# Cross-attention of a Perceiver layer: products for the row maxima in 64-row tiles, one bank for keys and values

## The reference

```python
q = query_states @ Wq.T + bq        # 128 rows, from layernorm(x)
k = key_value_states @ Wk.T + bk    # 12544 rows
v = key_value_states @ Wv.T + bv
# 16 heads of 16, q scaled by 1/4
scores = jnp.einsum('bhqd,bhkd->bhqk', q, k)
attn = jax.nn.softmax(scores, axis=-1)
ctx = jnp.einsum('bhqk,bhkd->bhqd', attn, v)
x = x + ctx @ Wo.T + bo
```

## Time and profile before

| | us |
|---|---|
| median of 3 runs | 610.64 |
| lowest and highest | 609.08, 611.08 |
| profiled execution | 610.5 |
| its span in the trace | 608.7 |

### The profile page before, as it was taken

The page is one execution under the profiler, slowest core; times in us unless marked ns, Lnnn a source line. Parts: engine busy times, 40 slices in busy tenths (PEclk is TensorE's granted clock), DMA queues, the critical chain, the costliest instruction groups (busy, mean ns, idle before and its releaser), DMA issues.

```text
span 608.7 us, 15724 instructions
## 1 busy us (share of the span) xinstructions
PE 550.2 (90%) x6337; PEld 490.0 (81%) x6337; DVE 432.7 (71%) x808; ACT 333.1 (55%) x629; POOL 91.7 (15%) x74
## 2 busy tenths in 40 slices
PE   3777999999999999999999999999999986364997
PEld 3776999999899999999989999998987874233886
DVE  5689877777777777777777777777784255574674
ACT  2311666666666666666666666666667730042563
POOL 6641110110110111111101101101000000006000
PEclk9889999999999999999999999999999996585899
DMA  7989866866867878878778768677583059700000
GB/s 258 139 135 137 139 108 110 128 111 109 128 113 110 123 116 115 118 116 118 116 110 125 113 109 127 110 111 101 85 133 116 4 184 376 269 1 1 1 1 9
DMA packets 44507, 70.46 MB, mean 116 GB/s; under 512 B 6772, under 2 KB 14868, under 8 KB 44308
## 3 DMA queue, kind: packets, MB, share of 16 engines
q1 hardware_dynamic: 44436, 69.47, 63.4%
HBM read 30.56 MB, written 0.13 MB: 50 GB/s over the span
## 4 chain that ended last, share of the span: by engine, by line
PE 79%; DVE 9%; DMA 5%; SPq 3%; issue 2%; ACT 1%; DVEq 0%
PE bank L558 18%; PE bank L575 16%; PE bank L537 14%; PE bank L524 10%; PE bank L509 10%; PE bank L747 4%; DMA kT<-kst 4%; PE bank L763 2%; PE bank L494 2%; SPq L239 2%; DVE stepmax L853 1%; PE bank L590 1%; DMA ctxT<-in_ctxT 1%; DMA qmat<-maxT 1%; PE bank L488 1%
## 5 line engine op out<-in xcount | busy, mean ns | idle before, releaser
L853 DVE TENSOR_REDUCE stepmax<-bank 128x2 f32<-128x512 f32 x392 | 267.6, 690 | 98.2 <-PE bank L537 68.7
L376 ACT ACTIVATE probs<-bank 128x512 f32<-128x512 f32 x392 | 231.5, 598 | 151.1 <-PE bank L558 149.7
L537 PE MATMUL bank<-kT,qM 128*128 128x256 f32 x784 | 160.7, 287 | 9.0 <-DMA kT<-kst 7.3
L558 PE MATMUL bank<-qmat,kT 128*128 128x256 f32 x784 | 165.7, 297 | 1.9 <-DMA qmat<-maxT 1.5
L558 PEld LDWEIGHTS bank<-qmat,kT 128*128 128x128 f32 x784 | 119.3, 191 | 23.1 <-issue 18.5
L537 PEld LDWEIGHTS bank<-kT,qM 128*128 128x128 f32 x784 | 122.2, 192 | 11.6 <-DMA kT<-kst 8.4
L309 POOL TENSOR_TENSOR cparts<-ctxT,cparts 128x512 fp32r<-128x512 f32 x49 | 63.0, 1286 | 350.0 <-ACT cparts L355 350.0
L524 PE MATMUL bank<-wv,cparts 128*128 128x256 f32 x588 | 103.5, 287 | 2.7 <-DVE maxT L878 2.7
L509 PE MATMUL bank<-cparts,wk 128*128 128x256 f32 x588 | 104.9, 290 | 0.0
L575 PE MATMUL bank<-probs,val 128*17 128x128 f32 x3136 | 104.7, 274 | 0.0
L524 PEld LDWEIGHTS bank<-wv,cparts 128*128 128x128 f32 x588 | 85.4, 195 | 4.7 <-issue 4.7
(11 more groups left out here) (176 smaller groups left out, 311.6 us busy)
## 6 DMA issues: line engine op xcount, KB each, us to landing
kT<-kst SPq DMA_DIRECT2D x294, 128.0 KB, 4.6
ctxT<-in_ctxT SPq DMA_DIRECT2D x49, 256.0 KB, 5.3
w<-in_w SPq DMA_DIRECT2D x24, 512.0 KB, 10.0
bias<-in_biases SPq DMA_DIRECT2D x1, 1024.0 KB, 7.8
qmat<-maxT SPq DMA_DIRECT2D x26, 8.0 KB
const<-in_const SPq DMA_DIRECT2D x1, 262.0 KB, 4.9
w_xk<-in_w_xk SPq DMA_DIRECT2D x1, 256.0 KB, 3.3
w_xv<-in_w_xv SPq DMA_DIRECT2D x1, 256.0 KB, 3.7
```

Source lines behind the costliest of these rows:

```text
L376: act.activation(probs[k % PROBS][:, :, :], sc_bank[k % 3][:, :].rearrange("p (h q) -> p h q", q=P), ACT.Exp).then_inc(S["exp_ready"], 1)
L537: last = pe.matmul(mx_bank[p % 2][:, a * SK:(a + 1) * SK], qM[:, p, a, :], kT[:, n % RING, p, :], start=True, stop=True)
L558: last = pe.matmul(sc_bank[k % 3][:, i * 2 * P:(i + 1) * 2 * P], kT[:, n % RING, p, j * P:(j + 1) * P], qmat[b % 2][:, p, :, :], start=Tru ...
L853: dve.tensor_reduce(stepmax[:, n % BS, 2 * p:2 * p + 2], mx_bank[p % 2][:, :].rearrange("p (a k) -> p a k", a=2), AX_X, ALU.max).then_inc( ...
```

## The change

1. A maximum product takes only the 64 rows of its half (`qM[rows, ...]`, `kT[rows, ...]`). Four products form a group `g`: head pairs `2g` and `2g + 1`, and for each the lower and the upper 64 rows. Half `a` writes to bank `a` of the pair of banks `wide[g % 2]`, pair `i` to half `i` of that bank. A group stands in slots 0, 2, 4 and 6. `mx_done` is raised twice a group.
2. `step_max` reduces 128 x 1024 columns of a pair of banks to four maxima, four times a round. `stepmax` has the shape `[P, BS, 2, PAIRS]`, and `block_max` reads it so.
3. Banks 0 to 3 are the two pairs, bank 4 holds keys and values in turn, banks 5 and 6 the scores, bank 7 stays. `keys` waits for `val_ready` of the step before and for `mt_read`, `values` waits for `kl_ready` of its own step; `scores` waits for the exponential two slots back.
4. All 12 key products stand in slots 2 and 3, all value products in slots 6 and 7. `turn_max` moves from slot 2 to slot 1, `values_out` on VectorE to the front of slot 0, `max_turned` from slot 3 to slot 1, `keys_low` from slot 5 to behind the reduction in slot 4.

The uses of the banks in the set-up move along (`xnT`, the query projection and `qT` to banks 0 to 3); those lines are left out here.

```diff
-        k_bank, v_bank, mx_bank, sc_bank, pv_bank = B[0], B[1], B[2:4], B[4:7], B[7]
+        wide = [ctx.enter_context(nc.psum_tensor(f"wide{i}", [P, 2, 512], F32)) for i in range(2)]
+        B = [wide[i // 2][:, i % 2, :] for i in range(4)]
+        B += [ctx.enter_context(nc.psum_tensor(f"bank{i}", [P, 512], F32))[:, :] for i in range(4, 8)]
+        k_bank, v_bank, sc_bank, pv_bank = B[4], B[4], B[5:7], B[7]
...
@@ keys
                     pe.wait_ge(S["cl_ready"], n + 1)
                     if n >= 1:
-                        pe.wait_ge(S["kl_ready"], n)
+                        pe.wait_ge(S["val_ready"], n)
+                    done = sum(last_step(b) <= n - 3 for b in range(NB))
+                    if done:
+                        pe.wait_ge(S["mt_read"], done)
@@ values
                 if (j, half) == (0, 0):
-                    if n >= 1:
-                        pe.wait_ge(S["val_ready"], n)
-                    done = sum(last_step(b) <= n - 3 for b in range(NB))
-                    if done:
-                        pe.wait_ge(S["mt_read"], done)
+                    pe.wait_ge(S["kl_ready"], n + 1)
@@ max_scores
-            def max_scores(n, p):
+            def max_scores(n, g):
-                m = 8 * n + p
-                if p == 0:
+                m = GROUPS * n + g
+                if g == 0:
                     pe.wait_ge(S[f"kt_load{n % 2}"], 96 * (n // 2) + 96)
                 if m >= 2:
                     pe.wait_ge(S["mx_read"], m - 1)
-                for a in range(2):
-                    last = pe.matmul(mx_bank[p % 2][:, a * SK:(a + 1) * SK], qM[:, p, a, :], kT[:, n % RING, p, :],
-                                     start=True, stop=True)
-                last.then_inc(S["mx_done"], 1)
+                for i in range(2):
+                    for a in range(2):
+                        rows = slice(64 * a, 64 * a + 64)
+                        last = pe.matmul(wide[g % 2][:, a, i * SK:(i + 1) * SK], qM[rows, 2 * g + i, a, :],
+                                         kT[rows, n % RING, 2 * g + i, :], start=True, stop=True)
+                        if i == 1:
+                            last.then_inc(S["mx_done"], 1)
@@ scores
-                if k >= 3:
-                    pe.wait_ge(S["exp_ready"], k - 2)
+                if k >= 2:
+                    pe.wait_ge(S["exp_ready"], k - 1)
...
@@ turn_part
-                if b == 0:
-                    pe.wait_ge(S["kl_ready"], NS)
-                if b == 1:
-                    pe.wait_ge(S["mt_read"], NB)
+                if b < 2:
+                    pe.wait_ge(S["mx_read"], GROUPS * NS)
@@ the rounds on TensorE
-                    if t < NS:
-                        max_scores(t, q)
-                    if q == 2:
+                    if q % 2 == 0 and t < NS:
+                        max_scores(t, q // 2)
+                    if q == 1:
                         for b in range(NB):
                             if t == last_step(b) + 1:
                                 turn_max(b)
                     if t + 2 < NS:
-                        if q < 4:
-                            keys(t + 2, q // 2, q % 2)
-                        else:
-                            values(t + 2, (q - 4) // 2, q % 2)
+                        if q in (2, 3):
+                            keys(t + 2, q - 2, 0)
+                            keys(t + 2, q - 2, 1)
+                        elif q in (6, 7):
+                            values(t + 2, q - 6, 0)
+                            values(t + 2, q - 6, 1)
@@ step_max
-                dve.wait_ge(S["mx_done"], 8 * n + p + 1)
-                dve.tensor_reduce(stepmax[:, n % BS, 2 * p:2 * p + 2],
-                                  mx_bank[p % 2][:, :].rearrange("p (a k) -> p a k", a=2), AX_X, ALU.max
+                dve.wait_ge(S["mx_done"], 2 * (GROUPS * n + g) + 2)
+                dve.tensor_reduce(stepmax[:, n % BS, :, 2 * g:2 * g + 2],
+                                  wide[g % 2][:, :, :].rearrange("p a (i k) -> p a i k", i=2), AX_X, ALU.max
                                   ).then_inc(S["mx_read"], 1)
@@ the rounds on VectorE
-                    if t < NS:
-                        step_max(t, q)
-                    if q == 1 and t + 1 < NS:
+                    if q == 0 and t + 1 < NS:
                         values_out(t + 1)
-                    if q == 3:
+                    if q % 2 == 0 and t < NS:
+                        step_max(t, q // 2)
+                    if q == 1:
                         for b in range(NB):
                             if t == last_step(b) + 1:
                                 max_turned(b)
-                    if q == 5 and t + 2 < NS:
+                    if q == 4 and t + 2 < NS:
                         keys_low(t + 2)
```

More of the change, by code:

```diff
@@ L127, in perceiver_layer @@
         xnT = sb("xnT", [P, DC, P])
-        stepmax = sb("stepmax", [P, BS, H])
+        stepmax = sb("stepmax", [P, BS, 2, PAIRS])
         curmax = sb("curmax", [P, H])
@@ L197, in perceiver_layer @@
         tparts = place("tparts", [P, 2, DC, P], F32R)
-        B = [ctx.enter_context(nc.psum_tensor(f"bank{i}", [P, 512], F32)) for i in range(8)]
-        k_bank, v_bank, mx_bank, sc_bank, pv_bank = B[0], B[1], B[2:4], B[4:7], B[7]
+        wide = [ctx.enter_context(nc.psum_tensor(f"wide{i}", [P, 2, 512], F32)) for i in range(2)]
+        B = [wide[i // 2][:, i % 2, :] for i in range(4)]
+        B += [ctx.enter_context(nc.psum_tensor(f"bank{i}", [P, 512], F32))[:, :] for i in range(4, 8)]
+        k_bank, v_bank, sc_bank, pv_bank = B[4], B[4], B[5:7], B[7]
         ident = const[:, C_ID:C_ID + P]
@@ L375, in exponential @@
                     act.wait_ge(S["pv_done"], (k - PROBS) // GROUPS + 1)
-                act.activation(probs[k % PROBS][:, :, :], sc_bank[k % 3][:, :].rearrange("p (h q) -> p h q", q=P),
+                act.activation(probs[k % PROBS][:, :, :], sc_bank[k % 2][:, :].rearrange("p (h q) -> p h q", q=P),
                                ACT.Exp).then_inc(S["exp_ready"], 1)
@@ L408, in _ @@
                             last = act.activation(qM[rows, PAIRS // 2:PAIRS, a, :],
-                                                  mx_bank[1][rows, :].rearrange("p (h q) -> p h q", q=P), ACT.Copy)
+                                                  B[3][rows, :].rearrange("p (h q) -> p h q", q=P), ACT.Copy)
                         last.then_inc(S["act_q0"], 1)
@@ L553, in scores @@
                     pe.wait_ge(S["max_rows"], 32 * (b + 1))
-                if k >= 3:
-                    pe.wait_ge(S["exp_ready"], k - 2)
+                if k >= 2:
+                    pe.wait_ge(S["exp_ready"], k - 1)
                 for i in range(2):
                     p = 2 * g + i
-                    last = pe.matmul(sc_bank[k % 3][:, i * 2 * P:(i + 1) * 2 * P], kT[:, n % RING, p, j * P:(j + 1) * P],
+                    last = pe.matmul(sc_bank[k % 2][:, i * 2 * P:(i + 1) * 2 * P], kT[:, n % RING, p, j * P:(j + 1) * P],
                                      qmat[b % 2][:, p, :, :], start=True, stop=True)
@@ L596, in _ @@
             pe.wait_ge(S["dve_xn"], 1)
-            transpose_d(xn, B[4], "pe_xnT")
+            transpose_d(xn, B[0], "pe_xnT")
             pe.wait_ge(S["dve_wkvl"], 1)
@@ L603, in _ @@
             pe.wait_ge(S["ld_q"], 32)
-            project(xnT, ["xq"], B[5]).then_inc(S["pe_q"], 1)
+            project(xnT, ["xq"], B[1]).then_inc(S["pe_q"], 1)
             pe.wait_ge(S["dve_wkvl"], 2)
@@ L612, in _ @@
                 for p in range(PAIRS // 2):
-                    last = pe.transpose(mx_bank[i][:, p * P:(p + 1) * P].bitcast(F32R),
+                    last = pe.transpose(B[2 + i][:, p * P:(p + 1) * P].bitcast(F32R),
                                         qparts[:, PAIRS // 2 * i + p, :, :, :].rearrange("q a s d -> q (a s d)"),
@@ L848, in values_out, with step_max @@
                                   ).then_inc(S["val_ready"], 1)
-            def step_max(n, p):
-                dve.wait_ge(S["mx_done"], 8 * n + p + 1)
-                dve.tensor_reduce(stepmax[:, n % BS, 2 * p:2 * p + 2],
-                                  mx_bank[p % 2][:, :].rearrange("p (a k) -> p a k", a=2), AX_X, ALU.max
+            def step_max(n, g):
+                dve.wait_ge(S["mx_done"], 2 * (GROUPS * n + g) + 2)
+                dve.tensor_reduce(stepmax[:, n % BS, :, 2 * g:2 * g + 2],
+                                  wide[g % 2][:, :, :].rearrange("p a (i k) -> p a i k", i=2), AX_X, ALU.max
                                   ).then_inc(S["mx_read"], 1)
             def block_max(b):
-                dve.wait_ge(S["mx_read"], 8 * last_step(b) + 8)
+                dve.wait_ge(S["mx_read"], GROUPS * last_step(b) + GROUPS)
                 count = last_step(b) + 1 - first_step(b)
-                dve.tensor_reduce(curmax[:, :], stepmax[:, 0:count, :].rearrange("p s h -> p h s"), AX_X, ALU.max
+                dve.tensor_reduce(curmax[:, :].rearrange("q (p a) -> q a p", a=2),
```

(7 more changed lines are left out.)

## The result

The changed kernel takes 635.5 us (634.75 to 636.22 in 4 runs) against 610.86 us in the same session: 1.039 times the time before, 95% interval 1.0357 to 1.0424. It is slower by 24.6 us; 630 us was forecast.

The account below looks back on a forecast made before the run. TensorE was taken to bound the full steps; +23.5 us (maximum groups) - 4.3 (block ends) + 1.5 (tail) - 1.0 (first steps) = +19.7 us, forecast 630 us. Its own range was 621 to 640 us; with rivals 1 and 2, 590 to 642 us.

Parts of the forecast that it names:

- What bounds: Steady steps: time is the number of TensorE instructions by their spacing; slack elsewhere is worth nothing.
- The price of a group: Maximum groups on TensorE, steps 5 to 46: 0.14 us more each, 0.56 us a step, +23.5 us.
- the middle value: Maximum group between full products: shape changes cost time, row halves run together; 0.74 us against 0.60 us.
- the 0.31 us: Change of tile shape on TensorE: 0.31 us between product starts instead of 0.12, read at the bursts of weighted values.
- VectorE: Reductions of 1024 columns: 1.18 us each, 4.7 us a step against 5.5; off the path, worth nothing by itself.
- The shared bank: Value products waiting for keys_low in full steps: released 0.1 us early, counted 0; 0.1 us a step kept for the range.
- The end of a block: Block steps: moved transpose and copy of the maxima save 0.43 us in each of ten, -4.3 us.
- The tail: Half steps at the end: with two score banks, second scores of pairs start about 0.1 us later; +1.5 us.
- The first rounds: Steps 0 to 4: keys_low some 0.5 us earlier behind fewer reductions, part lost in the transfer queue; -1 us.
- 1 (no emptying, 594 us): Maximum groups: halves run together, shape changes cost nothing; faster, 594 us; chance 0.20.
- 2 (row halves run like full ones, 618 us): Maximum groups: no pairing or emptying, waits for the shared bank become visible; 618 us; chance 0.14.
- 3 (halves in sequence): Maximum groups: emptying, and halves one after the other; +64 us from groups, 671 us; chance 0.13.

Follow-up runs that it names:

- four kernels with 6, 10, 12 and 18 changes: Row-half products grouped by eight, by four with two groups at bursts, as in the changed kernel, and by two; 590.2, 656.2, 635.5 and 711.2 us.
- full products: Changed kernel with maximum products over all 128 rows again, same groups, banks and order; 619.12 us, ratio 1.014 to the kernel before.
- full products and keys first: Changed kernel with 128-row maximum products, and keys_high before slot 4's exponential, keys_low before its reduction; 612.9 us, ratio 1.0027.
- idle products: Changed kernel with 14 idle products more in each of rounds 0 to 4; 633.61 us, ratio 1.0377.
- groups of eight: Changed kernel with keys first, row-half products in two groups of eight right before the bursts of weighted values; 590.2 us, ratio 0.9659.
- pairs: Changed kernel with keys first, the same row-half products in eight groups of two, one in each slot; 711.2 us.
- with a third score bank: Changed kernel with a third score bank from round 50 on, the bank of keys and values; 631.52 us, ratio 1.0348.
- with keys first: Changed kernel with keys_high before slot 4's exponential on ScalarE and keys_low before the third reduction on VectorE; 635.88 us, ratio 1.0401.
- all of it on the groups of eight: Groups of eight with the third score bank from round 50 on and 12 idle products more in each of rounds 0 to 4; 588.81 us, ratio 0.9637.
- fours, two at a burst: Changed kernel with keys first, groups of four in slots 1, 3, 5 and 7, two of them right before the bursts; 656.2 us.

## Why the prediction was right, point by point

**What bounds.** Right: between rounds 6 and 46 every 0.01 us of TensorE's step is in the end.

**The price of a group.** Right, with the middle value: 0.74 us was worked out, 0.74 us is in the rows, and the full step is 9.65 us as said. The step of the argument that could have failed was to carry the 0.31 us from column tiles over to row halves; four kernels with 6, 10, 12 and 18 changes now show it at 0.19 us above the normal spacing. The Trainium skill (TensorEngine Tiling (Array Packing), Key Properties) states that a change of the tiling mode drains TensorE, and also that different tiles can load and multiply in parallel. The runs agree with the first for row tiles too, by these four steps, though they show the price of a change and not the emptying itself; and with the second, by the four loads in 0.30 us and the four products in 0.50 us, where four full ones take 0.64 us. It takes both to know the sign. I had looked for an idle mark of 0.2 us at the group's loads; the gap is there between the starts, but no mark stands at it.

**VectorE.** 1224 ns for a reduction, 1180 were worked out.

**The shared bank.** No wait in the full steps, as counted, with 0.1 us of room: `keys_low` ends at 321.67, and the load of the first value product starts at 321.82.

```profile
320.80 0.87 DVE L840 SCALAR_TENSOR_TENSOR kst<-bank,kbias,kst 128x256 fp32r<-128x256 f32 x2
...
321.82 0.77 PEld L525 LDWEIGHTS bank<-wv,cparts 128*128 128x128 f32 x6
```

With full products in the same places it is 0.21 us of wait a step. In the first rounds, for which the prediction did not count this wait at all, TensorE waits for `keys_low` 10.5 us in six waits; the waits for the keys' transfer shrink there from 6.2 to 0.7 us, so that little of it shows.

**The end of a block.** Right: 0.14 us for a block step above a full one, 0.12 was counted (9.8 us said, 9.79 measured). One wait was not counted, that of the transposed maxima for `values_out`: it is just hidden here (the copy ends at 324.58, the load of the transpose starts at 324.70) and shows with full products and keys first, 0.17 us a block step. So the number is right with some luck.

**The tail: a term mis-sized.** +3.0 us for +1.5. I had followed one pair of score products and found 0.1 us. That price is about right where turned parts stand between the pairs: rounds 50 to 52 take 0.5 us more together. But 1.9 of the 3.0 us are in round 49 (6.8 us for 4.9) and 0.6 in the last. The changed kernel's rows in round 49, where no turned parts stand between the pairs, show nearly 0.5 us a pair instead:

```profile
487.74 0.50 PE L563 MATMUL bank<-qmat,kT 128*128 128x256 f32 x2 [0.45 <-ACT probs L378]
...
488.72 0.51 PE L563 MATMUL bank<-qmat,kT 128*128 128x256 f32 x2 [0.47 <-ACT probs L378]
```

**The first rounds: a term mis-sized, and one missed.** Most of the 5 us is here. The 1 us gained by earlier keys did not come (+0.2 us), and in round 5 the granted clock stood at 0.70: 11.35 us where 8.01 + 0.56 = 8.57 were due. I had costed this stretch by its order alone, not by what a half clock does when it reaches a round that TensorE bounds. In the kernel before, the half clock fell between 38 and 42 us, into rounds that wait anyway. What makes it fall where it does stays open: it moved between two kernels that do the same work there, and idle products went with a full clock in one kernel and not in the other.

**The rivals.** 1 (no emptying, 594 us) and 2 (row halves run like full ones, 618 us) fall with the group's rows. 2's number is near that of the kernel with full products (619 us), which is that case, but partly by luck: its wait was 0.21 us for 0.27, and the tail took 3 us more for the half put down for both ends. 3 (halves in sequence) falls with the four loads in 0.30 us.

## What to carry to other kernels

Before you use a part of the array for small products, count the changes of shape that this puts into TensorE's stream: here, with products of 256 columns, each cost 0.19 us, and each pair of row halves gave back 0.12 us against two full products. So gather products of one shape (groups of eight gained where groups of four lost and pairs lost more) and put groups of different small shapes next to each other, so that the way back to full shape is paid once. And look in the trace before for any change of shape at all: the two bursts of weighted values held the price of this edit.

## What the runs showed of the hardware

- The change from row halves to column tiles costs about as much as the change to full shape: the step of the groups of eight, worked out with 0.31, 0.22 and 0.31 us for the three changes around a burst, was met to 0.01 us. In its rows the last pair of the group starts at 303.64 + 0.10 + 3 x 0.12 = 304.10, and the first load of the burst at 304.31, again 0.21 us later.
- The half clock of the first rounds is not tied to one kernel. One profile of each:

| kernel | first score product, us | clock from 22 us to it | round 5, us | clock in it |
|---|---|---|---|---|
| before | 60.29 | 0.96 | 8.01 | 1.00 |
| full products | 59.83 | 1.00 | 8.34 | 1.00 |
| full products, keys first | 62.42 | 0.96 | 8.14 | 1.00 |
| the changed kernel | 60.46 | 0.95 | 11.35 | 0.70 |
| with a third score bank | 62.66 | 0.90 | 9.34 | 0.89 |
| with keys first | 64.14 | 0.90 | 9.35 | 0.89 |
| with idle products | 60.85 | 1.00 | 8.55 | 1.00 |
| groups of eight | 61.64 | 0.89 | 7.81 | 0.96 |
| all of it on the groups of eight | 63.30 | 0.89 | 7.50 | 1.00 |
| fours, two at a burst | 75.30 | 0.60 | 9.21 | 0.88 |
| pairs | 67.99 | 0.80 | 14.97 | 0.59 |

With products on 128 rows, round 5 ran at full clock each time; with row halves it did so in two kernels of eight, both with idle products. That is a hint and no more, as the changed kernel and the one with a third score bank do the same work up to there. Why the clock is so low with the fours at the bursts stays open.
